# Value products of two key tiles in three rounded passes, and a new order around the turn and the product of key tile 2

## The reference, cut to what matters

```python
q = rope((x @ Wq.T).reshape(b, n, H, D))
k = rope(jnp.einsum('bnd,bnh->bnhd', kp, kh))
v = jnp.einsum('bnd,bnh->bnhd', vp, vh)
scores = jnp.where(mask, jnp.einsum('bnhd,bmhd->bhnm', q, k) * scale, -jnp.inf)
p = jax.nn.softmax(scores, axis=-1)
o = jnp.einsum('bhnm,bmhd->bnhd', p, v).reshape(b, n, H * D)
return o @ Wout.T
```

## Time and profile before

| | |
|---|---|
| median of 3 runs | 772.39 us (771.72 to 772.47) |
| profiled execution, its own time | 773.12 us |
| its span (first to last instruction) | 771.3 us |
| mean granted PE clock over the span | 0.991 |
| busy share of the span: PE, DVE, ACT, POOL | 96%, 70%, 63%, 71% |
| chain that ended last, by engine | PE 79%, DVE 8%, idle that nothing explains 4%, ACT 3%, POOL 3% |
| attention loop, `first_turned` of unit 0 to that of unit 63 | 52.55 us to 565.32 us of the span |

### The profile page before, as it was taken

The page is one execution under the profiler, slowest core; times in us unless marked ns, Lnnn a source line. Parts: engine busy times, 40 slices in busy tenths (PEclk is TensorE's granted clock), DMA queues, the critical chain, the costliest instruction groups (busy, mean ns, idle before and its releaser), DMA issues.

```text
span 771.3 us, 13828 instructions
## 1 busy us (share of the span) xinstructions
PE 737.6 (96%) x4364; PEld 628.8 (82%) x4364; DVE 537.1 (70%) x1475; ACT 489.8 (63%) x1223; POOL 545.5 (71%) x459
## 2 busy tenths in 40 slices
PE   4799999999999999999999999999999999999993
PEld 4578888888888888888888888888878779998883
DVE  6976887776776766776777667777655427778577
ACT  5467877777676777776677876677753245555143
POOL 4467898878788887687799988689844064441774
PEclk9999999999999999999999999999999999999998
DMA  9411166422222121122122232122225043552343
GB/s 297 135 51 45 57 174 185 156 85 72 67 61 78 56 78 61 57 77 60 58 76 84 75 84 70 56 70 76 63 76 159 1 156 123 207 210 92 96 122 122
DMA packets 47747, 75.72 MB, mean 98 GB/s; under 512 B 9728, under 2 KB 24640, under 8 KB 47680
## 3 DMA queue, kind: packets, MB, share of 16 engines
q1 hardware_dynamic: 43504, 65.19, 27.7%
q0 software_dynamic: 3072, 8.39, 3.4%
q10 hardware_dynamic: 1104, 1.31, 0.5%
HBM read 57.71 MB, written 17.17 MB: 97 GB/s over the span
## 4 chain that ended last, share of the span: by engine, by line
PE 79%; DVE 8%; issue 4%; ACT 3%; POOL 3%; DMA 2%; ACTq 0%; DVEq 0%; POOLq 0%
PE ps L433 24%; PE ps L983 15%; PE ps L948 14%; PE ps L999 10%; PE ps L969 8%; PE ps L1146 5%; DVE stats L1374 1%; PE ps L1181 1%; ACT prob L634 1%; DVE q_sw L1328 1%; POOL o_lo L1816 1%; DMA kvh_rows<-hc_t 1%; PE ps L1208 1%; POOL slot_inputs L1832 1%; DVE stats L1267 1%
## 5 line engine op out<-in xcount | busy, mean ns | idle before, releaser
L634 ACT ACTIVATE prob<-ps,neg_max 128x512 f32<-128x512 f32 (+3 forms) x256 | 133.9, 527 | 44.6 <-DVE neg_max L1343 44.3
L1343 DVE CUSTOM_DVE_ANT_0 ps<-ps,causal_row 128x512 f32<-128x512 f32 (+3 forms) x256 | 120.4, 511 | 57.6 <-PE ps L948 57.5
L983 PE MATMUL ps<-pt,vp 128*128 128x512 f32 (+3 forms) x512 | 148.8, 434 | 0.0
L1797 POOL TENSOR_TENSOR q_sw<-q_cos,q_sw 128x512 f32<-128x512 f32 x62 | 79.3, 1280 | 76.3 <-DVE q_cos L1331 76.3
L983 PEld LDWEIGHTS ps<-pt,vp 128*128 128x128 f32 x512 | 82.5, 191 | 47.5 <-issue 30.1
L969 PE MATMUL ps<-id_f,prob 128*128 128x128 f32 x640 | 92.7, 276 | 1.4 <-ACT pt L643 1.4
L1816 POOL TENSOR_TENSOR o_lo<-o_t,o_hi 128x512 fp32r<-128x512 f32 x64 | 83.4, 1303 | 10.3 <-ACT o_hi L680 9.2
L948 PE MATMUL ps<-k_hi,q_hi 128*128 128x512 f32 x248 | 83.0, 335 | 1.9 <-ACT prob L634 1.7
L1806 POOL TENSOR_TENSOR k_lo<-kh_row,k_hi 128x512 fp32r<-128x512 f32 x62 | 80.0, 1290 | 5.0 <-ACT k_hi L668 5.0
L1801 POOL TENSOR_TENSOR q_lo<-q_sw,q_hi 128x512 fp32r<-128x512 f32 x62 | 80.3, 1295 | 2.4 <-ACT q_hi L674 2.4
L1811 POOL TENSOR_TENSOR kh_row<-kt,kh_row 128x512 f32<-128x512 f32 x62 | 80.9, 1305 | 0.0
(11 more groups left out here) (220 smaller groups left out, 1936.7 us busy)
## 6 DMA issues: line engine op xcount, KB each, us to landing
kh_row<-kvh_rows SPq DMA_DIRECT2D x64, 256.0 KB, 3.2
inv_row<-inverse_sums SPq DMA_DIRECT2D x64, 256.0 KB, 3.2
slot_inputs<-zeros SPq DMA_DIRECT2D x8, 640.0 KB, 5.1
xg<-slot_inputs SPq DMA_DIRECT2D x8, 640.0 KB, 4.8
slot_outputs<-yo SPq DMA_DIRECT2D x8, 640.0 KB, 3.3
up_raw<-in_w_up_dram SPq DMA_DIRECT2D x8, 368.0 KB, 4.8
wo_raw<-in_wout_dram SPq DMA_DIRECT2D x4, 512.0 KB, 8.0
dn_sb<-in_w_dn_dram SPq DMA_DIRECT2D x8, 256.0 KB, 3.6
```

Source lines behind the costliest of these rows:

```text
L634: ins = act.activation(prob[:, i % 2, ROW_AT[nt]:ROW_AT[nt] + w], ps_s[bank][:, at:at + w], ACT.Exp, scale=-1.0, bias=neg_max[:, i % 2, nt ...
L983: ins = pe.matmul(ps_o[:, mt * P:SEQ], vp[:, b * TPB + mt, :], pt[:, i % 2, cols], start=(mt == 0), stop=(mt == PT_BANKS[-1][-1]))
L1343: ins = dve.tensor_tensor_reduce(s_, s_, causal_row[:, (NT - 1 - nt) * P:], 1.0, BIG, ALU.add, ALU.min, neg_max[:, i % 2, nt:nt + 1])
L1797: pool.tensor_tensor(q_sw[:], q_cos[:], q_sw[:], ALU.add).then_inc(q_sum_ready, 1)
```

## The change

The products of key tiles 0 and 1 go from plain float32 to three rounded passes; tiles 2 and 3 stay as they are. For that:

- The values of key tiles 0 and 1 of each batch are split once per batch: ACT rounds them (`head_of_values`, 128 by 256) and POOL takes the residue (`rest_of_values`), for batch 0 ahead of the loop, for batches 1 to 3 in units 10, 26 and 42.
- ACT's copies of tiles 0 and 1 are written rounded (`pt_hi`). DVE writes their residues (`low_turned`, two instructions per unit, 512 and 384 columns) from PSUM, right behind `inverses(i+1)`. PE waits for them at the last two of the six passes.
- The turned tiles lose their second buffer; ACT and DVE wait for the value products of the unit before they write.
- PE's order is new: `weigh_values(i)` without tile 2 stands ahead of `turn_probs(i, [2])`, which waits for the residue of tile 0; tile 2's product (`weigh_last_tile`) stands behind `gather_output(i-1)`.
- ACT does `rest_turned(i)` behind `head_of_keys(i+3)`, and the last group of exponentials ahead of `head_of_output(i)`.
- `o_lo` loses its second buffer; POOL's `rest_of_output` waits for the output products of the unit before.

```diff
@@ ACT, turn i @@
-                rest_turned(i)
                 if i + 3 < UNITS:
                     head_of_keys(i + 3)
...
+                for b in range(1, B):
+                    if i == values_step(b):
+                        head_of_values(b)
+                rest_turned(i)
...
-                head_of_output(i)
                 if i + 2 < UNITS:
                     exps(i + 2, [2])
+                head_of_output(i)
@@ PE @@
                     if k == 0 and i:
                         pe.wait_ge(pt_rest_ready, i)
                     if k == 1 and i:
-                        pe.wait_ge(pt_second_ready, i)
+                        pe.wait_ge(pt_lo_ready, 2 * i)
...
                     if k == 2:
-                        pe.wait_ge(pt_first_ready, i + 1)
+                        pe.wait_ge(pt_lo_ready, 2 * i + 1)
...
-                for k, tiles in enumerate(PT_BANKS):
-                    pe.wait_ge((pt_first_ready, pt_second_ready, pt_rest_ready)[k], i + 1)
-                    for mt in tiles:
-                        cols = slice(COL_AT[mt], COL_AT[mt] + SEQ - mt * P)
-                        ins = pe.matmul(ps_o[:, mt * P:SEQ], vp[:, b * TPB + mt, :], pt[:, i % 2, cols],
-                                        start=(mt == 0), stop=(mt == PT_BANKS[-1][-1]))
-                ins.then_inc(o_psum, 1)
+                hi, lo = vs_hi[b % 2], vs_lo[b % 2]
+                pe.wait_ge(vs_ready, b + 1)
+                pe.wait_ge(pt_first_ready, i + 1)
+                pe.matmul(ps_o[:], hi[:, 0, :], turned(0), start=True, stop=False)
+                pe.matmul(ps_o[:], lo[:, 0, :], turned(0), start=False, stop=False)
+                pe.wait_ge(pt_second_ready, i + 1)
+                pe.matmul(ps_o[:, P:SEQ], hi[:, 1, :], turned(1), start=False, stop=False)
+                pe.matmul(ps_o[:, P:SEQ], lo[:, 1, :], turned(1), start=False, stop=False)
+                pe.matmul(ps_o[:, 3 * P:SEQ], vp[:, b * TPB + 3, :], turned(3), start=False, stop=False)
+                for mt in range(SPLIT):
+                    pe.wait_ge(pt_lo_ready, 2 * i + mt + 1)
+                    pe.matmul(ps_o[:, mt * P:SEQ], hi[:, mt, :], pt_lo[:, COL_AT[mt]:COL_AT[mt] + SEQ - mt * P],
+                              start=False, stop=False)
+
+            def weigh_last_tile(i):
+                pe.wait_ge(pt_rest_ready, i + 1)
+                pe.matmul(ps_o[:, 2 * P:SEQ], vp[:, batch(i) * TPB + 2, :], turned(2), start=False, stop=True).then_inc(o_psum, 1)
@@ PE, turn i @@
                     scores(i + 2, [0, 1])
+                weigh_values(i)
                 turn_probs(i, [2])
...
-                weigh_values(i)
...
                     gather_output(i - 1)
+                weigh_last_tile(i)
@@ DVE @@
+            def low_turned(i, mt):
+                if i:
+                    dve.wait_ge(o_psum, i)
+                dve.wait_ge((pt_first_ready, pt_second_ready)[mt], i + 1)
+                col = batch(i) * H + head(i)
+                bank, at = pt_slot(mt)
+                cols = slice(COL_AT[mt], COL_AT[mt] + SEQ - mt * P)
+                dve.scalar_tensor_tensor(pt_lo[:, cols], ps_pt[bank][:, at:at + SEQ - mt * P], vcol[:, mt, col:col + 1],
+                                         pt_hi[:, cols].bitcast(F32), ALU.mult, ALU.subtract).then_inc(pt_lo_ready, 1)
@@ DVE, turn i @@
                     inverses(i + 1)
+                for mt in range(SPLIT):
+                    low_turned(i, mt)
@@ POOL @@
+                if i:
+                    pool.wait_ge(proj_psum, i)
+                pool.tensor_tensor(o_lo[:], o_t[:], o_hi[:, i % 2, :].bitcast(F32), ALU.subtract) \
```

More of the change, by code:

```diff
@@ L156, in decoder_layer @@
         o_hi = place("o_hi", R2 + 64 * KB, [2, SEQ], F32R)
-        o_lo = place("o_lo", R2 + 68 * KB, [2, SEQ], F32R)
-        pt = place("pt", PT_AT, [2, PACKED])
+        o_lo = place("o_lo", R2 + 68 * KB, [SEQ], F32R)
+        SPLIT = 2
+        SPLIT_COLS = COL_AT[SPLIT]
+        pt_hi = place("pt_hi", PT_AT, [SPLIT_COLS], F32R)
+        pt_rest = place("pt_rest", PT_AT + SPLIT_COLS * 4, [PACKED - SPLIT_COLS])
+        pt_lo = place("pt_lo", PT_AT + PACKED * 4, [SPLIT_COLS], F32R)
+        vs_lo = [place(f"vs_lo{r}", R2 + (70 + r) * KB, [SPLIT, D], F32R) for r in range(2)]
         rope_sb = place("rope_sb", ROPE, [2 * SEQ])
@@ L261, in decoder_layer @@
         at_in, at_out = (small(n, [2, TILES], U32) for n in ("at_in", "at_out"))
+        vs_hi = [place("vs_hi0", PT_AT + (PACKED + SPLIT_COLS) * 4, [SPLIT, D], F32R), small("vs_hi1", [SPLIT, D], F32R)]
         id_in, rope_in, consts_in, w0_in = sem("id_in"), sem("rope_in"), sem("consts_in"), sem("w0_in")
@@ L349, in wo_head, with turned, values_step @@
             return i + WO_FIRST if i + WO_FIRST < H else None
+        def turned(mt):
+            at, w = COL_AT[mt], SEQ - mt * P
+            return pt_hi[:, at:at + w] if mt < SPLIT else pt_rest[:, at - SPLIT_COLS:at - SPLIT_COLS + w]
+        def values_step(b):
+            return H * b - 6
         def y_tile(b, t):
@@ L614, in values_of, with head_of_values @@
                 act.copy(vp[:, b * TPB:(b + 1) * TPB, :], ps[VALUE_BANK[b]][:]).then_inc(v_ready, 1)
+            def head_of_values(b):
+                act.wait_ge(v_ready, b + 1)
+                if b >= 2:
+                    act.wait_ge(o_psum, H * (b - 1))
+                act.copy(vs_hi[b % 2][:], vp[:, b * TPB:b * TPB + SPLIT, :]).then_inc(vs_hi_ready, 1)
             def head_of_wq(h0, h1):
@@ L639, in first_turned @@
                 act.wait_ge(pt_psum, 3 * i + 1)
-                if i >= 2:
-                    act.wait_ge(o_psum, i - 1)
+                if i:
+                    act.wait_ge(o_psum, i)
                 col = batch(i) * H + head(i)
-                act.activation(pt[:, i % 2, COL_AT[0]:COL_AT[0] + SEQ], ps_pt[0][:], ACT.Copy,
+                act.activation(turned(0), ps_pt[0][:], ACT.Copy,
                                scale=vcol[:, 0, col:col + 1]).then_inc(pt_first_ready, 1)
@@ L651, in second_turned @@
                     w = SEQ - mt * P
-                    ins = act.activation(pt[:, i % 2, COL_AT[mt]:COL_AT[mt] + w], ps_pt[bank][:, at:at + w], ACT.Copy,
+                    ins = act.activation(turned(mt), ps_pt[bank][:, at:at + w], ACT.Copy,
                                          scale=vcol[:, mt, col:col + 1])
@@ L660, in rest_turned @@
                 w = SEQ - mt * P
-                act.activation(pt[:, i % 2, COL_AT[mt]:COL_AT[mt] + w], ps_pt[bank][:, at:at + w], ACT.Copy,
+                act.activation(turned(mt), ps_pt[bank][:, at:at + w], ACT.Copy,
                                scale=vcol[:, mt, col:col + 1]).then_inc(pt_rest_ready, 1)
@@ L743, in _ @@
             values_of(0)
+            head_of_values(0)
             gates_of(1)
@@ L993, in gather_output @@
                 pe.wait_ge(o_hi_ready, i + 1)
-                for j, (w, o_) in enumerate(((wo_hi, o_hi), (wo_lo, o_hi), (wo_hi, o_lo))):
+                for j, (w, o_) in enumerate(((wo_hi, o_hi[:, r, :]), (wo_lo, o_hi[:, r, :]), (wo_hi, o_lo[:]))):
                     if j == 2:
@@ L1807, in rest_of_keys, with rest_of_values @@
                     .then_inc(k_lo_ready, 1)
+            def rest_of_values(b):
+                pool.wait_ge(vs_hi_ready, b + 1)
+                pool.tensor_tensor(vs_lo[b % 2][:], vp[:, b * TPB:b * TPB + SPLIT, :], vs_hi[b % 2][:].bitcast(F32),
+                                   ALU.subtract).then_inc(vs_ready, 1)
             def scale_keys(i):
@@ L1815, in rest_of_output @@
                 pool.wait_ge(o_hi_ready, i + 1)
-                pool.tensor_tensor(o_lo[:, i % 2, :], o_t[:], o_hi[:, i % 2, :].bitcast(F32), ALU.subtract) \
+                if i:
+                    pool.wait_ge(proj_psum, i)
+                pool.tensor_tensor(o_lo[:], o_t[:], o_hi[:, i % 2, :].bitcast(F32), ALU.subtract) \
                     .then_inc(o_lo_ready, 1)
@@ L1852, in _ @@
             rotate(1)
+            rest_of_values(0)
             scale_keys(2)
@@ L1879, in _ @@
                     scatters(b, i)
+                for b in range(1, B):
+                    if i == values_step(b):
+                        rest_of_values(b)
                 if i and wq_head(i - 1) is not None:
```

9 lines of the change are left out of this document (5 added, 4 removed).

## The result

The changed kernel takes **799.79 us** (median of 4 runs, 798.83 to 800.97), against 772.2 us of the kernel before in the same series: a ratio of 1.0359, 95% interval [1.0344, 1.0375], slower. The forecast was 788.5 with a range up to 801: the sign and the range held, the sum came out 11 us short. The profiled execution has a span of 798.4 us, granted PE clock 0.990.

The account below looks back on a forecast made before the run. PE was taken as the bound, its unit shrinking 0.295 us to 7.665, with the ring close behind. Terms +3.8, -3.2, +1.6, +1.9, +4.8, +0.4, +6.7, 0 sum to +16 on 772.4: 788.5 us, range 780 to 801.

Parts of the forecast that it names:

- the stages 3 to 5: Units 3 to 5: DVE's scan and weight residue before the sine product no longer hidden by PE's work; +3.8 us.
- 37 to 42: Units 37 to 42: already bound by the ring, DVE's extra work 8.1 us with gaps; +4.8 us.
- units 6 to 16 at 7.67: Eleven units gain PE's 0.295 us each, the path with the weight residue just inside at 7.5; -3.2 us.
- the residues' upper price: Rival: DVE's two residues cost 1.3 us, making the ring 7.77, above PE in every unit; 798 us, chance 0.15.
- the ring: Wait loop: DVE sine to cosine product, POOL's rotate, key residue, query residue, back to DVE; 7.57 us plus DVE's extra work.
- the extra work in the ring: DVE's work beyond a plain unit, between sine and cosine product: 7.1 us in units 17 to 29, 8.1 in 37 to 42.
- cancelled: Rival: stalls of units 3 to 5 and 30 to 34 are absorbed by slack elsewhere; 772 to 776 us, chance 0.05.
- units 17 to 29: Norms of the finished batch put 7.1 us into the ring, little of the lag paid back; 105.1 us, +1.6.
- units 43 to 45: Three units after the routing, one of them bound by the ring; +0.4 us.
- Units 30 to 36: Routing transpose, its copy and residue come after the late tile 2 product and output rounding; 61.2 us, +1.9.
- Units 59 to 63: Five gains of 0.295 us against one unpriced DVE weight split ahead of unit 62's residues, set at 1.5; sum 0.
- PE's saving prevails: Rival: the ring's extra work shrinks or moves, so DVE's idle time swallows the residues; 754 to 768 us, chance 0.08.

Follow-up runs that it names:

- the kernel with all moves: Changed kernel with rotary sum over the cosine product, DVE's extra work, weight residues and gate products behind the second maxima, quarter's residue behind the sine product: 791.71 us.

## Why the prediction was right, and where its sum was short

**Right:** that PE's gain would be lost in a loop through DVE, that the residues stand inside it (without them 771.7), the stages 3 to 5 (+3.7 against +3.8) and 37 to 42 (+4.8 both), and most of the signs named ahead: `q_lo` releases 27 sine products, where it was 12; PE waits for the residues ahead of the last passes; units 37 to 42 take 53.14 / 6 = 8.86. One sign failed: units 6 to 16 at 7.67.

**Luck in it:** the forecast's own band was 783 to 795, and 799.79 lies above it. The range reached 801 to make room for the residues' upper price, and that price did not come (the residues take 1.15 us of the ring, not 1.3). In units 37 to 42 two errors met: with a ring of 7.70 the same sum gives 6 x 7.70 + 8.1 - 0.4 = 53.9, and the extra work in the ring came to 7.0 instead of 8.1 (the six periods exceed 7.70 by that). The range also leaves out all of *cancelled* (772 to 776), not most of it.

**Short,** term by term, 11 us in all:
- *Ring 7.57, PE 7.665.* They are 7.70 and 7.73. The residues took 1.15 instead of 1.10, the cosine product 0.68 instead of 0.65, POOL's three instructions 0.04 more, and PE's gain was 0.23. Each is a few hundredths, but the forecast lived on their difference: it paid lag back at 0.095 us a unit, and there are 0.03. The extra work in the ring of units 17 to 29 was well sized (7.1; the periods of units 17 to 27 exceed 7.70 by 6.8 in sum). With 7.70 and 7.73 the forecast's own sum gives 13 x 7.73 + 7.1 - 13 x 0.03 - 0.4 = 106.8 there, 1.7 of the 2.4 us that were missing; what the other 0.7 is, no run singles out. In units 43 to 45 and 53 to 58 together 0.6 were missing. The paragraph of the Trainium skill that spoke for a higher price ("VectorE: DVE Perf Modes", section "The DRAIN you can't avoid") goes on that "A next op that is not held starts earlier". The trace agrees with that sentence: the two residues take 1.24 us from the first start to the second end, and the cosine product starts 1.15 after the first start.
- *Units 6 to 16, the weight residue at 0.8.* It was taken from unit 3, and "just inside" at 7.5 us turned out just outside, at 7.90. At the start of turn 13 it runs beside POOL, in order of time, DVE and POOL:

```profile
164.31 1.20 DVE L1410 TENSOR_TENSOR wo_lo<-wo_raw,wo_hi 128x256 fp32r<-128x256 f32 x1
165.53 0.69 DVE L1363 TENSOR_TENSOR q_sw<-ps,rope_sb 64x512 f32<-64x512 f32 x1
```

```profile
163.92 1.29 POOL L1849 TENSOR_TENSOR q_lo<-q_sw,q_hi 128x512 fp32r<-128x512 f32 x1
```

  It ends 0.3 us behind the end of `q_lo`, and the sine product follows at once. In the kernel with all moves it takes 0.42, started 0.05 ahead of POOL, and these units take 85.03:

```profile
144.33 0.42 DVE L1414 TENSOR_TENSOR wo_lo<-wo_raw,wo_hi 128x256 fp32r<-128x256 f32 x1
144.38 1.52 POOL L1861 TENSOR_TENSOR k_lo<-kh_row,k_hi 128x512 fp32r<-128x512 f32 x1
```

  1.9 us were missing here, of which PE's smaller gain makes 11 x 0.065 = 0.7.
- *Units 30 to 36,* 1.0 us, and as much in units 46 to 52: unit 36 had been put at 8.2, and its step from sine to sine product took 9.1, since unit 37 begins with a copy of the logits that waits for PE. The trace before already had 9.4 for that step.
- *Units 59 to 63,* put at zero with the remark that no row had the price of DVE's split of a weight. That was an oversight: the trace before has it at 559.38, 1.38 and 1.76 us. In the changed kernel it ends at 584.99, ahead of unit 62's residues, and that unit takes 7.08 instead of 5.30. Behind the loop another 2.0 us are lost: the last unit's division starts 5.72 us after ACT's copy of tile 0 instead of 4.31, since tile 2's product stands behind the output products there too, with no later unit to cover it; the other 0.6 is not placed. 4.6 us in all.

The ring was the right place and not the whole cause: it is one of two loops that share DVE's stretch between sine and cosine product. The forecast's number hardly depends on that, since the second is 0.3 us shorter; the rival "PE's saving prevails" did: it named moved extra work as its condition, and with it moved the time came to 779, not below 772; the routing, which grows beside POOL, had to stay inside.

## What to carry to other kernels

When a loop of waits nearly equals the bound, work out both to the hundredth, or treat the difference as zero: such hundredths made about a quarter of the missing sum. Before a loop is named as the cause, ask which other loops pass through the same stretch of the same engine; cutting one of two gave 0.3 us a unit, moving the extra work out of the stretch that they share gave 4.4 us in units 17 to 29. And a price taken from one row holds only for the neighbours of that row: what POOL does at that time belongs to the price of a DVE instruction.

## What the runs showed of the hardware

DVE instructions with two inputs in SBUF and POOL instructions ran one after the other. The weight residue took 0.42 us where it began ahead of POOL's instruction (POOL's then took 1.52 instead of 1.30) and 0.5 to 1.6 behind its start; `slot` 0.17 and 0.93; the product over the gates 0.69 and 1.43. With one input in SBUF it differed: a norm of 256 columns took 0.37 to 0.41 alone and 1.48 beside POOL, but the two instructions of the inverses kept 0.18 and 0.31 beside it. DVE instructions with an input in PSUM kept their time beside POOL: the division 0.69, the first maxima 0.69. The Trainium skill states this in "SBUF — State Buffer", section "SBUF: two separate sides": DVE in a two-port mode or with two SBUF inputs and GpSimd share a port pair under an exclusive lock, and whoever starts first has it for the whole instruction. The rows with two inputs agree, in both directions; in which mode the norm runs, no row shows. The forecast had not looked there.
